# TensorE's column registers two tiles at a time, pad transfers spread over four loads, GpSimd's norm ahead of its row work, and late sums after the last tiles

## The reference

```python
x = x + xattn(layernorm(x), ctx, ctx, Wq, bq, Wk, bk, Wv, bv, Wo, bo)
x = x + ffn(layernorm(x), conf_w, conf_b, gate_w, up_w, down_w, wealth)

# xattn: 16 heads of 8, linear attention over the positions
qp, kp = elu(q) + 1, elu(k) + 1
sums_t = sum over s <= t of outer(kp_s, v_s)        # causal
res_t  = sums_t applied to qp_t;  Z = cumsum(qp, axis=1)
out    = (res / Z) @ Wo + bo

# ffn: 8 experts, the best 2 of each token
bids    = sigmoid(x @ conf_w.T + conf_b) * wealth
top_bids, selected = top_k(bids, 2)
weights = softmax(top_bids)
expert(x) = down_w @ (silu(gate_w @ x) * (up_w @ x))
output  = sum over the 2 selected experts of weight * expert(x)
```

## Time and profile before

| what | value |
|---|---|
| time, median of 3 runs | 331.06 us (330.39 to 331.72) |
| the profiled execution | 329.64 us |
| its span | 327.9 us |
| PE busy | 296.4 us, 90% |
| DVE busy | 263.0 us, 80% |
| ACT busy | 234.5 us, 72% |
| POOL busy | 203.0 us, 62% |
| mean granted TensorE clock | 0.986 |

### The profile page before, as it was taken

How to read it: one execution, slowest core, us unless ns; L and a number is a source line. 1 busy time by engine, 2 the same in 40 slices (tenths; PEclk the granted TensorE clock), 3 DMA queues, 4 the chain that set the end, 5 groups by cost and what they waited for, 6 DMA issues and landing times.

```text
span 327.9 us, 12647 instructions
## 1 busy us (share of the span) xinstructions
PE 296.4 (90%) x4611; PEld 245.1 (75%) x4611; DVE 263.0 (80%) x721; ACT 234.5 (72%) x468; POOL 203.0 (62%) x304
## 2 busy tenths in 40 slices
PE   7888998997999999799599999999999899999970
PEld 5467685775768686676289989988999899899930
DVE  6699999998999999788777697989567566666763
ACT  3698896988798897957259777667667577677620
POOL 5672333687878789788567657877554345444530
PEclk9999999999999999999899999999999999999996
DMA  7231413333243422401264334587959657533895
GB/s 215 81 105 57 128 37 88 108 100 110 81 116 101 128 78 53 130 30 42 49 105 72 64 67 93 161 175 195 171 156 207 185 160 155 83 67 109 269 309 190
DMA packets 49034, 39.59 MB, mean 121 GB/s; under 512 B 32710, under 2 KB 39756, under 8 KB 48976
## 3 DMA queue, kind: packets, MB, share of 16 engines
q1 hardware_dynamic: 43648, 28.62, 34.6%
q0 software_dynamic: 4320, 8.47, 9.7%
q10 hardware_dynamic: 1008, 1.70, 1.5%
HBM read 15.29 MB, written 12.21 MB: 84 GB/s over the span
## 4 chain that ended last, share of the span: by engine, by line
PE 38%; DVE 24%; POOL 10%; issue 9%; SPq 7%; DMA 6%; ACT 5%; POOLq 0%; DVEq 0%; ACTq 0%
DVE Pm L1108 5%; POOL by_expert L644 4%; PE bank L1676 4%; PE scores L1678 3%; PE scores L1676 3%; PE bank L1677 3%; PE scores L1677 3%; PE bank L1678 3%; PE bank L1697 3%; PE bank L1698 3%; PE bank L1705 3%; DVE Vexp L1081 2%; SPq L541 2%; DVE w_both L1175 2%; DVE Z L1089 2%
## 5 line engine op out<-in xcount | busy, mean ns | idle before, releaser
L644 POOL DMA_INDIRECT by_expert<-token_rows,rows_to x64 | 68.3, 1067 | 22.2 <-issue 17.9
L772 POOL DMA_INDIRECT by_token<-y_sb,row_meta x55 | 56.8, 1032 | 40.6 <-ACT y_sb L960 29.3
L1377 DVE SCALAR_TENSOR_TENSOR hid<-scores,silu 128x512 f32<-128x512 f32 x71 | 48.0, 689 | 30.8 <-PE scores L1678 27.4
L976 ACT ACTIVATE hid_hi<-hid 128x512 f16<-128x512 f32 x71 | 44.2, 628 | 20.1 <-DVE hid L1377 19.3
L969 ACT ACTIVATE silu<-bank 128x512 f32<-128x512 f32 x71 | 42.0, 596 | 22.1 <-PE bank L1678 20.0
L1383 DVE TENSOR_TENSOR Kexp<-hid,hid_hi 128x512 f16<-128x512 f32 x71 | 47.8, 688 | 8.0 <-ACT hid_hi L976 4.2
L1697 PE MATMUL bank<-w_both,hid_hi 128*128 x248 | 34.7, 219 | 2.2 <-issue 2.2
L1508 PEld LDWEIGHTS scores<-qT,Kexp 32*128 32x128 f32 x1024 | 31.4, 186 | 6.7 <-issue 6.7
L1508 PE MATMUL scores<-qT,Kexp 32*128 32x128 f32 (+1 forms) x1024 | 35.8, 276 | 0.0
L1698 PE MATMUL bank<-w_both,hid_hi 128*128 x248 | 34.5, 219 | 0.0
L1108 DVE TENSOR_SCALAR Pm<-scores 128x768 f32<-128x768 f32 x32 | 30.5, 954 | 2.5 <-PE scores L1508 2.1
(11 more groups left out here) (405 smaller groups left out, 789.7 us busy)
## 6 DMA issues: line engine op xcount, KB each, us to landing
w_raw<-in_w_pack_dram SPq DMA_DIRECT2D x24, 256.0 KB, 2.7
x_all<-in_x_tok_dram SPq DMA_DIRECT2D x8, 256.0 KB, 2.8
cT<-in_ctx_t_dram SPq DMA_DIRECT2D x8, 256.0 KB, 3.1
w_raw<-w_both SPq DMA_DIRECT2D x2, 768.0 KB, 3.9
Pm<-w_both SPq DMA_DIRECT2D x2, 768.0 KB, 5.1
Vexp<-w_both SPq DMA_DIRECT2D x2, 768.0 KB, 3.8
single_more<-w_both SPq DMA_DIRECT2D x2, 768.0 KB, 5.3
out_dram<-x_all ACTq DMA_DIRECT2D x6, 256.0 KB, 3.3
```

The source lines that it names most:

```text
L644: pool.indirect_dma_start(by_expert, bass.IndirectOffsetOnAxis(ap=rows_to[u % 2][:, s, b:b + 1], axis=0), token_rows[u % 2][:, b, s, :], N ...
L772: pool.indirect_dma_start(by_token, bass.IndirectOffsetOnAxis(ap=number, axis=0), y_sb[:, k, s, :], None, bounds_check=NT * TOP - 1, oob_i ...
L1377: dve.scalar_tensor_tensor(hid[:, slot, :], bank[2 + slot], 1.0 / WSCALE, silu[:, slot, :], ALU.mult, ALU.mult).then_inc(hid_done, 1)
```

## The change

Four edits, with no change to what is computed.

- `TURN` is 2 in place of 8: 20 register loads of three values in place of five of nine.
- `pad()` takes a list of experts. It is called ahead of `load_tile` 11, 12, 13 and 14 for two experts each, in place of all eight ahead of `load_tile(13)`. The wait for pad_at now stands ahead of `load_tile(11)`.
- GpSimd's body has `tail(u - 1)` ahead of `tail_rows(u - 2)` for units 2 to 6. In the last body the order is as it was.
- DVE runs all tile steps and then all the sums of `DVE_OUTS`.

```diff
--- before.py
+++ after.py
@@ -503,9 +503,9 @@
             pad_rows = pad_row[:].unsqueeze(1).to_broadcast([P, TB, ROW])
             sp.dma_start(by_expert[E * REGION:E * REGION + TT, :].rearrange("(s p) r -> p s r", s=TB), pad_rows).then_inc(padded, 16)
 
-            def pad():
+            def pad(experts):
                 sp.wait_ge(pad_at_done, 1)
-                for e in range(E):
+                for e in experts:
                     at = sp.value_load(pad_at[0:1, e:e + 1], min_val=e * REGION, max_val=e * REGION + NT)
                     sp.dma_start(by_expert[bass.ds(at, TT), :].rearrange("(s p) r -> p s r", s=TB), pad_rows).then_inc(padded, 16)
 
@@ -526,8 +526,9 @@
                     sp.wait_ge(full_table, FULL_TABLE)
                     for rows in dispatched:
                         sp.wait_ge(rows, 16 * UB * TOP * FULL_UNITS // 2)
-                if i == FULL - 3:
-                    pad()
+                if FULL - 5 <= i < FULL - 1:
+                    j = 2 * (i - FULL + 5)
+                    pad(range(j, j + 2))
                 if i == FULL:
                     sp.wait_ge(padded, 16 * (E + 1))
                     sp.wait_ge(table, ROWS_AT)
@@ -652,12 +653,13 @@
                 pool.tensor_tensor(unit_start[:], unit_start[:], unit_ids[:], ALU.add).then_inc(id_next, 1)
 
             def body(u, par):
-                if u >= 2:
+                if last(u):
                     tail_rows(u - 2, par)
-                if last(u):
                     dispatch(u - 2, [0])
                 if not first(u):
                     tail(u - 1)
+                if u >= 2 and not last(u):
+                    tail_rows(u - 2, par)
                 if u == UNITS - 2:
                     dispatch(u - 2, range(UB))
                 elif u >= 2 and not last(u):
@@ -1429,14 +1431,8 @@
                 xu = x_all[:, u * UB:(u + 1) * UB, :]
                 dve.tensor_tensor(xu, xu, y_back[u][:, :, 1, :], ALU.add).then_inc(out_done, 1)
 
-            for i in range(TILES - LAST_SINGLES):
-                tile_step(i, i % 4)
-            for i, u in zip(range(TILES - LAST_SINGLES, TILES), DVE_OUTS):
-                hidden(i, i % 4, 0)
-                add_first(u)
-                low(i, i % 4, 0)
-                add_second(u)
-            for u in DVE_OUTS[LAST_SINGLES:]:
+            tiles(dve, tile_step)
+            for u in DVE_OUTS:
                 add_first(u)
                 add_second(u)
             for n, batches in enumerate(HALVES):
@@ -1735,7 +1731,7 @@
                         all_count()
                 return more if following else None
 
-            TURN = 8
+            TURN = 2
             assert FULL % TURN == 0 and TILES % TURN == 0
             pe.wait_ge(wlo_done, 3 * E)
             pe.wait_ge(full_table, FULL_TABLE)
```

## The result

| | before | changed |
|---|---|---|
| time, median of 4 runs | 331.07 us (330.39 to 331.72) | 338.54 us (336.89 to 340.81) |
| the profiled execution, its span | 329.64, 327.9 us | 338.25, 336.5 us |
| ratio, 95% interval | | 1.0227 (1.018 to 1.0274) |

The account below looks back on a forecast made before the run. VectorE bounds attention, GpSimd sets the tiles' start, TensorE and SP bound the tiles. First tile 5.3, tiles 3.0 (pads 3.3 less registers 0.3) and sums 0 make 8.3 us on 331.06: 339.4 us, range 333.5 to 342.5.

Parts of the forecast that it names:

- Waits that go, units 1 to 6: Attention: norm first removes VectorE stalls, 1.57 us in unit 1, 0.91 and 0.22 in unit 3, 1.62 in unit 6.
- Collisions, 1.85 us per unit: Attention units 2 to 6: GpSimd's two moved subtractions take turns with VectorE's four scans, costing VectorE 1.85 us per unit.
- rival of one collision in two: Attention: only one of two subtractions collides with the scans, 1.15 us per unit, 336.6 us total; no separate chance given.
- First tile +5.3: Attention to tiles: unit 5's last scatter, SP's first load and the first tile come 5.3 us later.
- Pads +3.3, at tile 31: Tiles: loads 11 and 12 behind the pad_at wait delay later loads; tile 31's gate and up start 3.3 us later.
- Register loads -0.3: TensorE in the tiles: shorter register loads remove idles, of which 0.3 us remains as gain.
- Up to 16 more idles of 0.1: TensorE in the tiles: the bound on loss from more register loads, 1.6 us, of which none was taken.
- Late sums 0: VectorE at the end: moving ten additions behind the tiles costs zero, bounds -0.2 to 0.5 us.

Follow-up runs that it names:

- pad_wait_at_11: Kernel before with only the wait for pad_at moved, from ahead of load 13 to ahead of load 11: 335.41 us against 331.38, ratio 1.0113.
- sums_only: Kernel before with all of VectorE's sums behind the last tile and nothing else: 329.77 us against 330.38, ratio 0.9983.
- late_scans_and_turns_16: Kernel before with norm first, scans behind the subtractions, and registers loaded for 7, 8, 16 and 9 tiles: 334.78 us against 328.83, ratio 1.0197.
- norm_only: Kernel before with GpSimd's norm ahead of its row work in units 2 to 6 and nothing else: 334.68 us against 330.38, ratio 1.0166.
- turn_only: Kernel before with registers loaded for two tiles at a time and nothing else: 333.26 us against 330.38, ratio 1.0146.

## Why the forecast held, step by step

- **Waits that go, units 1 to 6**: right. VectorE's statistics of unit 2 came 1.56 us earlier (forecast 1.57), those of unit 3 0.31 later (0.28), `place` took 0.23, and VectorE's idles of units 3 and 6 are gone.
- **Collisions, 1.85 us per unit**: right in kind, wrong in size. The price of one is 0.91 (2.28 less 1.37), and units 3 to 5 pay one, not two. Unit 2 paid the 1.85 (3.21 less 1.36), though the forecast's own working doesn't give it: 0.45 + 1.15 + 0.34 + 1.15 + 0.34 ends at 3.43, not near 3.2, and costs 2.06. The step that failed is "the next instruction about 0.17 later, at 37.46": I took the `shift` from unit 1, where it took 0.20 us beside the scans. In units 3 to 5 it took 0.44, and this 0.24 us put one subtraction past the scans. My rival of one collision in two was the better guess for them.
- **First tile +5.3**: measured +4.4, by two errors. VectorE's lag at unit 6 was 1.7 and not 4.7 us. But GpSimd took 1.2 us more from there to the last scatter instead of 0.9 less, all of it in unit 6. Its subtractions took 2.56 in place of 2.29, the numbers of its rows 0.65 in place of 0.21, its eight scatters 0.3 more. Another 0.5 are pauses between the numbers and the first scatter, where the four instructions of the norm stood before. `shift` and `rstd` gave back 0.35. I had let VectorE pay for collisions and GpSimd not, and the order itself had no price.
- **Pads +3.3, at tile 31**: wrong in size and place. Loads behind the wait were the cause, as forecast (`pad_wait_at_11`). The failed step is that the lead would carry the lateness to tile 31, and tiles 11 to 14 would share about the 0.8 us of before. The lead was 13.3 us at load 11; the wait of 8.8 us left 4.6, and loads among pad transfers took 5 to 6 us from issue to use, so TensorE waited at once, and 5.1 us were gone by tile 16. The trace of before held the hint: load 13 was issued at 212.2, and tile 13 waited until 217.8 (the wait is in the earlier trace rows), so there was no lead at all at that tile. The term itself was too small as well: load 15 came 6.0 us later against the first tile, not 3.3, since beside the two loads the issues among the pads took longer, load 13's 2.43 us in place of 1.2 and load 11's small one 1.59 in place of 0.4. The waits that I had expected at tiles 19 to 31 didn't come.
- **Register loads -0.3**: wrong, about +1 to +2. I had covered a third of the length everywhere; TensorE had 1.15 us queued behind a single tile and 0.8 behind a wait, the loads took up to 1.36 and 1.72 us there, and idles of up to 0.5 and of 1.2 us show. "Up to 16 more idles of 0.1" (it is 15 more loads) was too low a bound.
- **Late sums 0**: right (`sums_only`).
- **The end**: not in the sum, 2.0 us back, open.

Too much for the collisions and too little for the pads and registers lay within a microsecond of each other. The direction came from mechanisms that the runs confirm; that the total missed by only 0.9 us was luck.

## What to carry to other kernels

Before an instruction is moved on one engine, look at what the others run at its new place: here each collision in SBUF cost the bound engine 0.91 us, most of the other's instruction of 1.3, and a quarter of a microsecond decided how many there were. Moving the victim (here the scans) can do as well as moving the culprit. A wait put further ahead in a busy queue delays all the transfers behind it. Read from the trace how far ahead of their use these are issued now, and compare that with the wait plus the slowest landing nearby, not the median one. Small loads in a sequencer's stream are free only where the work queued ahead of them outlasts them.

## What was not expected of the hardware

- Behind a wait of 4.72 us TensorE's granted clock was 0.5 for more than 4 us (`pad_wait_at_11`), and the tile that followed took 2.3 us longer; where the waits were 2.47 and 1.34 us in the changed kernel it stayed at 1.00. Behind the idle of 4.3 us in `late_scans_and_turns_16` it was 0.53 from 229 to 232 us, which is part of that run's loss.
- The first tile shows the same: it took 5.1 us before, 5.4 in the changed kernel and 4.0 in `norm_only`, by how long the clock stayed at 0.5 (`turn_only`, with 1.00 throughout, took 3.7). So a microsecond or more comes and goes with it from one execution to the next.
- A register load of 17 values took TensorE 5.35 us, one of 3 values 0.77 to 1.8.
